# A triangle norm in two halves, scan neighbours over 96 columns, and routing maxima of unscaled exponentials

## What is computed

```python
# triangle, over a 128x128 grid, 16 channels
z = jnp.einsum('bikc,bkjc->bijc', a, b)
return g * (_ln(z, ln2_g, ln2_b) @ Wz + bz)
...
# scan, row by row; K = 9 taps, 64 columns
new = row + jax.nn.relu(conv1d_same(carry, W))
...
# experts: softmax over 512 tokens, the top 8 per expert
probs = jax.nn.softmax(logits, axis=1)
vals, idx = jax.lax.top_k(probs.transpose(0, 2, 1), K)
pooled = jnp.einsum('bked,bke->bed', gathered, topv)
```

## Time and profile before

| | us |
|---|---|
| median of 3 runs | 390.98 (390.59 to 391.6) |
| the profiled execution's own time | 391.77 |
| its span, first to last instruction | 390.0 |
| busy: PE, DVE, ACT, POOL | 352.6, 228.8, 190.6, 33.0 |
| share of the chain that ended last: PE, ACT, DVE | 60%, 16%, 15% |

### The profile page before, as it was taken

The page is one execution under the profiler, slowest core; times in us unless marked ns, Lnnn a source line. Parts: engine busy times, 40 slices in busy tenths (PEclk is TensorE's granted clock), DMA queues, the critical chain, the costliest instruction groups (busy, mean ns, idle before and its releaser), DMA issues.

```text
span 390.0 us, 9515 instructions
## 1 busy us (share of the span) xinstructions
PE 352.6 (90%) x4074; PEld 233.3 (60%) x4074; DVE 228.8 (59%) x456; ACT 190.6 (49%) x414; POOL 33.0 (8%) x39
## 2 busy tenths in 40 slices
PE   7967999999998999998898999799998899999891
PEld 2434565656545899956555379257645654774691
DVE  2679967767758503156746764753446357245885
ACT  2859678979748400043942656440345306014461
POOL 0024712212120001000000100000000000000000
PEclk9999999999999999999999999999999799999997
DMA  8990000000430000020000000000000000000004
GB/s 224 164 209 33 2 2 3 2 4 2 97 69 0 3 3 3 3 57 2 0 2 2 0 3 2 2 0 2 2 2 0 0 2 0 3 2 1 2 0 110
DMA packets 7338, 9.91 MB, mean 25 GB/s; under 512 B 3694, under 2 KB 6398, under 8 KB 6910
## 3 DMA queue, kind: packets, MB, share of 16 engines
q1 hardware_dynamic: 5630, 8.23, 10.0%
q10 hardware_dynamic: 1664, 1.05, 0.9%
HBM read 6.65 MB, written 1.05 MB: 20 GB/s over the span
## 4 chain that ended last, share of the span: by engine, by line
PE 60%; ACT 16%; DVE 15%; issue 6%; DMA 2%; SPq 0%; DVEq 0%; ACTq 0%
PE bank L649 26%; PE bank L1077 6%; PE bank L274 6%; PE bank L268 4%; PE bank L1007 3%; PE bank L1018 3%; ACT lnv L373 2%; PE bank L849 2%; DMA xR<-in_x 2%; PE bank L873 2%; ACT arena L1242 2%; DVE arena L1749 1%; ACT attn_scratch L1211 1%; ACT arena L1244 1%; ACT rs L378 1%
## 5 line engine op out<-in xcount | busy, mean ns | idle before, releaser
L367 ACT ACTIVATE sq<-bank 128x512 f32<-128x512 f32 x33 | 19.4, 592 | 67.6 <-PE bank L268 50.9
L649 PE MATMUL bank<-sb_consts 128*128 128x512 f32 (+1 forms) x94 | 43.0, 573 | 1.6 <-ACT arena L1442 1.6
L649 PE MATMUL bank<-xn,sb_w_attn 128*128 128x512 f32 x64 | 34.6, 622 | 6.8 <-ACT attn_scratch L1211 4.3
L274 PE MATMUL bank<-sq,sb_consts 128*128 128x512 f32 x66 | 34.6, 610 | 0.5 <-ACT sq L367 0.2
L373 ACT ACTIVATE lnv<-bank 128x512 f32<-128x512 f32 x33 | 19.7, 597 | 30.5 <-PE bank L274 30.2
L649 PE MATMUL bank<-arena 64*32 64x256 f32 (+4 forms) x466 | 26.7, 382 | 3.6 <-ACT arena L1244 2.2
L1077 PEld LDWEIGHTS bank<-arena,sb_w_late 128*128 128x128 f32 x180 | 23.0, 191 | 11.1 <-DVE arena L1808 8.0
L1077 PE MATMUL bank<-arena,sb_w_late 128*128 128x128 f32 x180 | 27.2, 287 | 1.7 <-DVE arena L1808 1.3
L1018 PE MATMUL bank<-arena,sb_w_late 128*128 128x128 f32 x144 | 27.9, 276 | 0.0
L1007 PE MATMUL bank<-arena,sb_consts 128*128 128x128 f32 x144 | 27.7, 276 | 0.1
L1379 ACT ACTIVATE arena<-bank 128x128 f32<-128x128 f32 x72 | 20.0, 278 | 13.9 <-PE bank L1018 13.8
(11 more groups left out here) (209 smaller groups left out, 621.7 us busy)
## 6 DMA issues: line engine op xcount, KB each, us to landing
arena<-in_w_spec SPq DMA_DIRECT2D x2, 720.0 KB
sb_w_late<-in_w_late SPq DMA_DIRECT2D x1, 1100.5 KB, 24.4
arena<-arena SPq DMA_DIRECT2D x4, 256.0 KB, 4.6
arena<-fourier SPq DMA_DIRECT2D x1, 768.0 KB, 22.2
sb_w_attn<-in_w_attn SPq DMA_DIRECT2D x1, 641.0 KB, 9.6
xR<-in_x SPq DMA_DIRECT2D x4, 128.0 KB, 4.0
xR<-in_x ACTq DMA_DIRECT2D x4, 128.0 KB, 4.2
arena<-in_w_spec SPq DMA_DIRECT2D x2, 256.0 KB
```

The source lines that it names most:

```text
L274: pe.matmul(bank[:, var_bank(i), :], mean32, sq[:, i % 2, :], start=True, stop=True)\
L367: act.activation(sq[:, i % 2, :], bank[:, centre_bank(i), :], ACT.Square).then_inc(S("ln_squared"), 1)
L649: return mm(ps, lhsT, rhs, start=True, stop=True)
```

## The change

It has three parts. The triangle norm works on each bank of 512 columns by itself: every semaphore of the chain counts to two, ACT's table change stands between the two copies, the scaling of the weights stands behind the second sum of squares, and filler there is three matmuls, not six. In the scan the middle shift still covers 128 columns and comes first; the two neighbour shifts cover the 96 columns that they reach, so the padding groups, POOL's two memsets and DVE's wait for them go. In the experts DVE finds and replaces the maxima of the unscaled exponentials, ACT writes the scaled block to `pm`, and DVE keeps the entries whose place was replaced by 0 (`is_equal`, then multiply); the token banks are copied in two halves between other work; one filler matmul ahead of the first share and the one ahead of the first pooling half go.

```diff
@@ -42,5 +42,5 @@
 BUSY = {2: 2, 3: 6, 4: 1, 5: 1, 7: 0}
-BUSY_ATTN, BUSY_TRI, BUSY_SCAN, BUSY_LOGITS = 4, (2, 2, 6, 1), 3, 2
+BUSY_ATTN, BUSY_TRI, BUSY_SCAN, BUSY_LOGITS = 4, (2, 2, 3, 1), 3, 2
 BUSY_ROW, BUSY_START, BUSY_BACK = 1, 3, 1
-BUSY_EXPERTS = (3, 1, 1, 3)
+BUSY_EXPERTS = (2, 1, 1, 3)
 WX_EARLY = [1, 2]
@@ -628,5 +628,2 @@
             pool.wait_ge(S("x_tri"), CH)
-            link(pool.memset(carry[:, :, 0, :], 0.0))
-            link(pool.memset(carry[:, :, 5, :], 0.0))
-            pool.sem_inc(S("edges"), 1)
             def guess(i):
@@ -953,13 +950,15 @@
                 last = pe.transpose(bank[:, 4 + m // 4, (m % 4) * P:(m % 4 + 1) * P], z_cols[:, m * P:(m + 1) * P], ident)
-            last.then_inc(S("z_ps"), 1)
+                if m % 4 == 3:
+                    last.then_inc(S("z_ps"), 1)
             full(bank[:, 6, 0:1], wz_rows, b2).then_inc(S("bz_ps"), 1)
             keep_busy(BUSY_TRI[2], 7)
-            pe.wait_ge(S("z_n"), 1)
             pe.wait_ge(S("bz2"), 1)
             for m in range(8):
+                pe.wait_ge(S("z_n"), m // 4 + 1)
                 last = pe.transpose(bank[:, 6 + m // 4, (m % 4) * P:(m % 4 + 1) * P], zn[:, m * P:(m + 1) * P],
                                     ident)
-            last.then_inc(S("z_tr"), 1)
+                if m % 4 == 3:
+                    last.then_inc(S("z_tr"), 1)
             keep_busy(BUSY_TRI[3], 4)
-            pe.wait_ge(S("z_t"), 1)
+            pe.wait_ge(S("z_t"), 2)
             pe.wait_ge(S("wz_g"), 1)
@@ -1075,5 +1074,5 @@
                     pe.wait_ge(S("row_done"), H * i + h)
-                    for w in range(3):
-                        last = mm(bank[:, 4 + h % 2, 0:P], band[i][:, w, :], carry[:, h - 1, w:w + 4, :],
-                                  start=(w == 0), stop=(w == 2))
+                    for w, (lo, hi) in ((1, (0, 4)), (0, (1, 4)), (2, (0, 3))):
+                        last = mm(bank[:, 4 + h % 2, B * lo:B * hi], band[i][:, w, :], carry[:, h - 1, w + lo:w + hi, :],
+                                  start=(w == 1), stop=(w == 2), skip_group_check=True)
                     last.then_inc(S("row_ps"), 1)
@@ -1116,3 +1115,4 @@
                                             xmQ[:, g, h * P:(h + 1) * P], ident)
-                last.then_inc(S("xtok_ps"), 1)
+                    if g % 4 == 3:
+                        last.then_inc(S("xtok_ps"), 1)
                 keep_busy(BUSY_EXPERTS[0], 7)
@@ -1127,4 +1127,4 @@
                     last.then_inc(S("pmt_ps"), 1)
-                    pe.wait_ge(S("xtok"), 1)
-                    keep_busy(BUSY_EXPERTS[1], 3)
+                    pe.wait_ge(S("xtok"), half + 1)
+                    keep_busy(BUSY_EXPERTS[1] * half, 3)
                     pe.wait_ge(S("pmt"), half + 1)
@@ -1354,3 +1354,2 @@
             act.activation(gate[:, :], bank[:, 0:4, :], ACT.Sigmoid, bias=bg).then_inc(S("gate"), 1)
-            lnexp()
             for k in range(2):
@@ -1358,9 +1357,15 @@
                 act.activation(flat(z_cols, k), bank[:, 4 + k, :], ACT.Copy).then_inc(S("z_cols_sb"), 1)
-            act.wait_ge(S("z_c"), 1)
-            act.activation(zq[:, :], zc[:, :], ACT.Square).then_inc(S("z_sq"), 1)
-            act.wait_ge(S("z_var"), 1)
-            link(act.activation(zst[:, 2, :], zst[:, 1, :], ACT.Ln, bias=LN_TOK, scale=1.0 / CT))
-            act.activation(zst[:, 3, :], zst[:, 2, :], ACT.Exp, scale=-0.5).then_inc(S("z_rstd"), 1)
-            act.wait_ge(S("z_tr"), 1)
-            act.activation(zT[:, :], bank[:, 6:8, :], ACT.Copy).then_inc(S("z_t"), 1)
+                if k == 0:
+                    lnexp()
+            for k in range(2):
+                act.wait_ge(S("z_c"), k + 1)
+                act.activation(flat(zq, k), flat(zc, k), ACT.Square).then_inc(S("z_sq"), 1)
+            for k in range(2):
+                act.wait_ge(S("z_var"), k + 1)
+                of_half = slice(32 * k, 32 * k + 32)
+                link(act.activation(zst[:, 2, of_half], zst[:, 1, of_half], ACT.Ln, bias=LN_TOK, scale=1.0 / CT))
+                act.activation(zst[:, 3, of_half], zst[:, 2, of_half], ACT.Exp, scale=-0.5).then_inc(S("z_rstd"), 1)
+            for k in range(2):
+                act.wait_ge(S("z_tr"), k + 1)
+                act.activation(flat(zT, k), bank[:, 6 + k, :], ACT.Copy).then_inc(S("z_t"), 1)
             ln_act(act, LN_RNN)
@@ -1430,3 +1435,8 @@
                 act.wait_ge(S("moe_sum"), j + 1)
-                act.activation(ex[:, j, :], ex[:, j, :], ACT.Copy, scale=mo[:, 8 + j:9 + j]).then_inc(S("moe_share"), 1)
+                act.activation(pm[:, j, :], ex[:, j, :], ACT.Copy, scale=mo[:, 8 + j:9 + j]).then_inc(S("moe_share"), 1)
+            def expert_tokens(half):
+                act.wait_ge(S("xtok_ps"), half + 1)
+                act.activation(xtok[:, 4 * half:4 * half + 4].rearrange("p g h n -> p (g h n)"),
+                               bank[:, 2 * half:2 * half + 2, :].rearrange("p k n -> p (k n)"), ACT.Copy).then_inc(S("xtok"), 1)
 
@@ -1439,7 +1449,7 @@
             expert_share(2)
-            expert_share(3)
-            act.wait_ge(S("xtok_ps"), 1)
-            act.activation(xtok.rearrange("p g h n -> p (g h n)"), bank[:, 0:4, :].rearrange("p k n -> p (k n)"), ACT.Copy).then_inc(S("xtok"), 1)
+            expert_tokens(0)
             act.wait_ge(S("pmt_ps"), 1)
             act.activation(pmt[:, 0:2].rearrange("p j h n -> p (j h n)"), bank[:, 6, :], ACT.Copy).then_inc(S("pmt"), 1)
+            expert_share(3)
+            expert_tokens(1)
             act.preload_act_table_set("gelu_and_others")
@@ -1668,19 +1678,31 @@
 
-            dve.wait_ge(S("z_ps"), 1)
-            zp = bank[:, 4:6, :].rearrange("p k n -> p (k n)").rearrange("p (q c j) -> p q j c", q=NQ, c=CT)
-            z4 = [a.rearrange("p (q j c) -> p q j c", q=NQ, j=16) for a in (zc, zq, zn)]
-            link(dve.tensor_reduce(out=zst[:, 0, :], in_=zp, axis=AX, op=ALU.add))
-            link(dve.tensor_scalar(zst[:, 0, :], zst[:, 0, :], -1.0 / CT, None, ALU.mult))
-            zm = zst[:, 0, :].rearrange("p (q j o) -> p q j o", q=NQ, o=1).to_broadcast([P, NQ, 16, CT])
-            dve.tensor_tensor(z4[0], zp, zm, ALU.add).then_inc(S("z_c"), 1)
+            def by_row(a):
+                return a.rearrange("p (q c j) -> p q j c", q=2, c=CT)
+            def of_rows(a):
+                return a.rearrange("p (q j c) -> p q j c", q=2, c=CT)
+            def spread_rows(a, k):
+                return a[:, 32 * k:32 * k + 32].rearrange("p (q j o) -> p q j o", q=2, o=1).to_broadcast([P, 2, 16, CT])
+            for k in range(2):
+                dve.wait_ge(S("z_ps"), k + 1)
+                zs = zst[:, 0, 32 * k:32 * k + 32]
+                link(dve.tensor_reduce(out=zs, in_=by_row(bank[:, 4 + k, :]), axis=AX, op=ALU.add))
+                link(dve.tensor_scalar(zs, zs, -1.0 / CT, None, ALU.mult))
+                dve.tensor_tensor(of_rows(flat(zc, k)), by_row(bank[:, 4 + k, :]), spread_rows(zst[:, 0, :], k), ALU.add)\
+                    .then_inc(S("z_c"), 1)
             dve.wait_ge(S("bz_ps"), 1)
             dve.tensor_tensor(bz2[:, :], bank[:, 6, 0:1], bz, ALU.add).then_inc(S("bz2"), 1)
+            for k in range(2):
+                dve.wait_ge(S("z_sq"), k + 1)
+                dve.tensor_reduce(out=zst[:, 1, 32 * k:32 * k + 32], in_=of_rows(flat(zq, k)), axis=AX, op=ALU.add)\
+                    .then_inc(S("z_var"), 1)
             dve.tensor_scalar(wz[:, :, :], wz[:, :, :], g2, None, ALU.mult).then_inc(S("wz_g"), 1)
-            dve.wait_ge(S("z_sq"), 1)
-            dve.tensor_reduce(out=zst[:, 1, :], in_=z4[1], axis=AX, op=ALU.add).then_inc(S("z_var"), 1)
-            dve.wait_ge(S("z_rstd"), 1)
-            zr = zst[:, 3, :].rearrange("p (m o) -> p m o", o=1).to_broadcast([P, 64, CT])
-            dve.wait_ge(S("z_c"), 1)
-            dve.tensor_tensor(zn.rearrange("p (m c) -> p m c", c=CT), zc.rearrange("p (m c) -> p m c", c=CT), zr,
-                              ALU.mult).then_inc(S("z_n"), 1)
+            for k in range(2):
+                dve.wait_ge(S("z_rstd"), k + 1)
+                dve.wait_ge(S("z_c"), k + 1)
+                dve.tensor_tensor(of_rows(flat(zn, k)), of_rows(flat(zc, k)), spread_rows(zst[:, 3, :], k), ALU.mult)\
+                    .then_inc(S("z_n"), 1)
 
@@ -1789,3 +1811,2 @@
                 ln_dve(dve, k, lambda q, n: ln_apply_r(dve, q, n))
-                dve.wait_ge(S("edges"), 1)
                 dve.wait_ge(S("ln_applied"), ln_at(k + 1))
@@ -1837,6 +1858,7 @@
 
                 expert_sum(0)
-                expert_sum(1)
                 for j in range(4):
-                    dve.wait_ge(S("moe_share"), j + 1)
+                    if j < 3:
+                        expert_sum(j + 1)
                     link(dve.max(mo[:, 16 + 8 * j:24 + 8 * j], ex[:, j, :]))
@@ -1844,5 +1866,5 @@
                                            in_values=ex[:, j, :], imm_value=0.0))
-                    if j < 2:
```

(5 more changed lines are left out.)

## The result

The changed kernel takes **386.21 us**, the median of 4 runs (384.44 to 387.44), against 391.29 (390.59 to 391.88, 4 runs) for the kernel before beside it: a drop of 5.08 us. The ratio on record is 0.9858, with a 95% interval of 0.9823 to 0.9893 (the quotient of the two medians is 0.987). That is faster by more than the 0.3% that can be told; the prediction was 386.4, in a range from 384.6 to 389.0. The profiled execution took 385.72 us, its span is 383.9 us.

What follows compares the result with a forecast made beforehand. No engine bounds the whole; each edited stage is judged by its last waits. 391.77 - 2.0 - 2.1 - 0.5 = 387.2 us for the profiled execution, 0.8 us above the median, so 386.4 us; range 384.6 to 389.0.

Steps and rivals of the forecast that it cites:

- The triangle term: Triangle norm worked in halves: output matmuls start at 205.6 us where it was 207.62, a saving of 2.0 us.
- The line-up: Triangle norm: predicted engine-by-engine schedule of both halves, with DVE as the bound and output starting at 205.6 us.
- the 8 to 8.6 that was named as the sign: Triangle: sign of being right, output matmuls starting 8 to 8.6 us after the product ends.
- One sign of being wrong: Triangle: ACT's second copy, or the scaling of the weights, ending a wait of PE would count against the forecast.
- The experts term: Experts: earlier first maximum and token copy in halves bring pooling half 2 to 299.3 from 301.46, saving 2.1 us.
- The scan term: Scans: weight loads set the distance between passes; only the last pass's tail shrinks, 0.03 us in 20 rows, -0.5 us.
- Passes priced by columns: Rival in the scans: passes cost by their columns, saving the full 3.6 us; total 383.3 us, chance 0.04.
- The price of a fall: PE's granted clock: one fall to 0.50 like that from 306.6 to 313.4 costs 2.4 us.
- the chance of 0.18: Rival: one more fall of the clock in the thinned triangle or experts stretch, costing 2.4 us; 388.8 us, chance 0.18.
- the fall at 306.6 goes away: Rival: the clock's fall at 306.6 vanishes as the work ahead of it shifts; 384.0 us, chance 0.09.
- Halves that do not overlap: Rival in the triangle: DVE becomes the bound and the first term is 0; 388.4 us, chance 0.05.
- slower: Rival: the clock falls in both thinned stretches, each as long as before, costing 6.8 us; 393.2 us, chance 0.04.

Runs made afterwards that it cites:

- the scan part alone: The kernel before with only the scan edits (neighbour shifts over 96 columns, no padding memsets or wait on them): 389.45 us, ratio 0.9964.
- the experts part alone: The kernel before with only the experts' edits (maxima of unscaled exponentials, token copy in halves, two filler matmuls fewer): 388.80 us, ratio 0.9938.

## Why the prediction was right

**The sum.** Forecast -2.0, -2.1 and -0.5 us; the stages show -2.40, -2.19 and -0.58, together -5.17 where -4.6 was said.

**The triangle term** was 0.4 us too small. The line-up has the right order and the right bound: DVE, nearly unbroken in its first half. Two sizes were off in the same direction. DVE's operations, each 0.69 us long, follow at a shorter distance where one does not need the other's result: the sum over half 1 enters the chain with 0.61 us, and half 1 was subtracted at 200.89, not 201.05. Scaling the weights took 0.34 us, not 0.41. With these DVE multiplied half 0 until 203.15, not 203.6, the transposes started at 203.28, and output at 205.24 where 205.6 was said. Ln and Exp were quicker too (0.49 us from the start of the one to the end of the other, not 0.55), but were done before DVE was free in both accounts and set nothing. The distance from the end of the product is 8.1 us, in the 8 to 8.6 that was named as the sign. One sign of being wrong did show: ACT's second copy of z ends a wait of PE, of 0.27 us, at 197.96. The line-up itself had that wait (197.75 to 197.9), and it costs nothing, since DVE is on half 0 until 199.36.

**The experts term** held at each place (above, to 0.06 us), but not for the reason that its first steps suggest. It began with the earlier first maximum; the run with that alone gains 0.08 us. The gain needs the token halves, which with less filler give 1.79 us without it.

**The scan term** held: 0.29 us in each scan is 10 rows at 0.03, the 20 rows in all that were counted; the working gives 0.6, which went into the sum as 0.5. The distance between passes is 0.11 us and not 0.12, since the 0.74 us of six loads are five distances and the last load's own 0.19. The Trainium skill (TensorE: Matmul & The Clock Gate, Part 2: What happens when you issue a matmul) has the throughput of the streaming phase go by the number of columns alone. Where each pass brings new weights of 128x128, the distance between passes does not follow that here: six loads take 0.74 us with 128 columns in all passes, with 96 in four of them and with 32 in all, and only the last pass's tail follows the columns. Another section of the same page of the Trainium skill, LDWEIGHTS (loading the stationary operand), has a formula for the time of a weight load by its own columns; for 128 of them it gives an estimate of 107 ns. The rows agree, with their distance of 0.11 us whatever streams. *Passes priced by columns* is refuted.

**The clock.** The price of a fall was put at 2.4 us for one of 6.8 us. The way to the second scan takes 24.5 to 24.6 us with no fall (24.45 to 24.62 in four traces) and 27.07 with that one: 2.5 to 2.6. Falls of 3.4 us there cost 1.1 to 1.4 (six traces, 25.62 to 25.88, against 24.51). The changed kernel's trace has no fall in either thinned stretch, but one in the experts in another run with the same edit there: the chance of 0.18 was not idle. The rival that the fall at 306.6 goes away came half true, shorter by 3.4 us. That is no merit of the change: with the scan part alone, too, it was 3.4 us long (308.2 to 311.6). So the profiled executions' difference, 6.05 us, holds about 1.0 of clock (-1.45 and +0.47) that the stages of the change do not claim. For an execution like the profiled one 387.2 was forecast and 385.72 measured, 1.5 us apart: the triangle's 0.4 us too little and the clock's share lie on the same side. The closeness of the median, 0.2 us, is in part luck. Between the medians the drop is 5.08 us, 0.5 more than forecast, and the kernel before came out at 391.29 beside the change, 0.3 us above the 390.98 from which the forecast started.

**Halves that do not overlap** and **slower** are refuted by the chain and by the interval of the ratio.

## What to carry to other kernels

Splitting a chain in which engines take turns in two halves paid here until one engine's operations stood end to end; line up the halves engine by engine from measured durations, and the gain comes out to a few tenths of a us. An edit's worth depends on which wait it leaves as the last one, so two edits of one stage are measured apart and together. Where stretches of lower clock scatter the total by some us, compare the lengths of stages between the same instructions first, and the medians after.

## What the runs showed that was not expected

With 32 columns in each pass of the scan the granted clock fell to 0.50 at 262.6 and stayed there for 30.7 us, with PE busy for all of the 26.80 us of the stretch shown; with 96 columns in four of six passes it was 1.00 throughout both scans. A loss of 11.4 us in one scan (32.42 against 20.99) thus stood behind an edit whose rows, at full clock, are 0.05 us faster in DVE's wait. That the edit is the cause is not shown. It is one trace, and the kernel with the new maxima alone, whose scans are unedited, was at 0.50 for 20.5 us from 298.2. For the edit speaks that the clock fell 5.6 us into the first scan and 4.9 us into the second. Five filler matmuls of 128 columns, where PE had stood idle for 0.30 and 0.70 us ahead of two groups, went with a clock of 1.00 in a stretch that six other traces show at 0.50 for 3.4 us, but two without this filler at 1.00. A single trace of each of the two kernels that have it does not settle it. The mean clocks of their 11 runs, 0.985 to 0.989, against 0.975 to 0.983 in the 11 runs of the kernel before beside them, speak for the filler; against it, the ten runs of the experts part alone, without it, reach from 0.973 to 0.989.
